# Spreading the zero fill of three pair tables and starting a scatter stream later, in a four-layer graph network

## What is computed

```python
# layer 0, with h = layernorm(x)
msg = relu(h[src] + edge_attr @ We + be)
agg = segment_sum(msg, dst, num_segments=2500)
out = relu(batchnorm((h + agg) @ W + b))
# later layers use the same edges again (list 1), for example
out = segment_sum(h[src] * norm[:, None], dst, num_segments=2500)
# the expert network of layer 2 has attention over the second edge list (list 2)
```

## Time and profile before

| | |
|---|---|
| median of three timed runs | 6236.67 us |
| the profiled execution | 6194.75 us, span 6192.9 us |
| mean granted TensorE clock | 0.877 |
| TensorE busy | 4971.2 us (80%) |
| VectorE busy | 3507.4 us (57%) |
| GpSimd busy | 3159.1 us (51%) |
| ScalarE busy | 1631.4 us (26%) |
| row adds (L776) in the edge stage | 340, the first at 52.5 us, the last at 1465.4 us |

### The profile page before, as it was taken

How to read it: one execution, slowest core, us unless ns; L and a number is a source line. 1 busy time by engine, 2 the same in 40 slices (tenths; PEclk the granted TensorE clock), 3 DMA queues, 4 the chain that set the end, 5 groups by cost and what they waited for, 6 DMA issues and landing times.

```text
span 6192.9 us, 70248 instructions
## 1 busy us (share of the span) xinstructions
PE 4971.2 (80%) x23435; PEld 2959.7 (48%) x23497; DVE 3507.4 (57%) x7225; ACT 1631.4 (26%) x2765; POOL 3159.1 (51%) x2151
## 2 busy tenths in 40 slices
PE   4677767675999888989569796386775998999999
PEld 3444444444555675567566564383222333222266
DVE  5566666654566312120335410399996999777754
ACT  1111111112222102210232211126773001666521
POOL 4578888888888778877778778302220000000000
PEclk8777777776899989999778798698998999999999
DMA  7766666675544785569898776794443110322200
GB/s 203 160 130 117 118 123 113 122 107 65 17 16 13 66 97 16 17 54 110 119 148 100 57 75 39 115 210 111 112 111 79 29 29 21 82 81 81 79 14 27
DMA packets 534579, 523.31 MB, mean 85 GB/s; under 512 B 263641, under 2 KB 489874, under 8 KB 527159
## 3 DMA queue, kind: packets, MB, share of 16 engines
q1 hardware_dynamic: 271560, 427.90, 31.3%
q0 software_dynamic: 261696, 90.13, 23.3%
q10 hardware_dynamic: 1028, 1.52, 0.1%
HBM read 365.58 MB, written 153.75 MB: 84 GB/s over the span
## 4 chain that ended last, share of the span: by engine, by line
POOL 29%; PE 22%; DMA 19%; issue 16%; DVE 10%; SPq 4%; ACT 1%; DVEq 0%; POOLq 0%; ACTq 0%
POOL pairs L724 23%; DMA pairs<-PAIR_CNT,PAIR_IDX 11%; PE PS L2346 6%; PE PS L2183 5%; DMA sums<-WORK,XT 4%; SPq L187 4%; DVE MXS L2224 4%; DVE WORK L1987 4%; POOL sums L776 4%; POOL WORK L763 3%; DMA WORK<-x_table,WORK 3%; PE PS L1011 2%; PE PS L983 2%; PE PS L2204 2%; DVE WORK L1993 1%
## 5 line engine op out<-in xcount | busy, mean ns | idle before, releaser
L724 POOL DMA_INDIRECT pairs<-PAIR_CNT,PAIR_IDX x1364 | 2152.9, 1578 | 563.5 <-issue 421.7
L776 POOL DMA_INDIRECT sums<-WORK,XT x340 | 530.3, 1560 | 213.1 <-issue 113.0
L601 PE MATMUL PS<-WORK,IDENT 125*125 125x256 f32 x680 | 303.0, 538 | 405.9 <-DMA WORK<-x_table,WORK 405.3
L516 DVE SCALAR_TENSOR_TENSOR XT<-PS,ROWS 128x512 f32<-128x512 f32 x704 | 482.6, 746 | 182.7 <-PE PS L502 182.5
L2417 DVE SCALAR_TENSOR_TENSOR WORK<-WORK 125x1000 f32<-125x1000 f32 x400 | 462.3, 1197 | 152.7 <-ACT WORK L2385 151.9
L2183 PE MATMUL PS<-ROWS 32*125 32x500 f32 x3200 | 451.1, 633 | 28.9 <-DVE MXS L2224 19.3
L2224 DVE TENSOR_REDUCE MXS<-PS 125x4 f32<-125x2000 f32 x200 | 438.8, 2235 | 22.4 <-PE PS L2204 18.4
L1627 PE MATMUL PS<-IDENT,WORK 125*125 125x125 f32 x1920 | 259.8, 305 | 238.0 <-DMA WORK<-pairs 159.4
L1661 DVE CUSTOM_DVE_ANT_0 ROWS<-ROWS 125x1250 f32<-125x1250 f32 x200 | 280.8, 1457 | 299.5 <-ACT ROWS L1647 299.5
L644 ACT ACTIVATE WORK<-PS 125x256 f32<-125x256 f32 x340 | 131.0, 385 | 1193.5 <-PE PS L601 1193.5
L2385 ACT ACTIVATE WORK<-PS 125x1000 f32<-125x1000 f32 x400 | 380.0, 1002 | 239.3 <-PE PS L2334 239.3
(11 more groups left out here) (338 smaller groups left out, 8094.6 us busy)
## 6 DMA issues: line engine op xcount, KB each, us to landing
WORK<-pairs SPq DMA_DIRECT2D x400, 218.8 KB
pairs<-ROWS SPq DMA_DIRECT2D x75, 976.6 KB, 7.0
WORK<-pairs SPq DMA_DIRECT2D x48, 1093.8 KB
WORK<-pairs SPq DMA_DIRECT2D x80, 546.9 KB
pairs<-PAIR_CNT,PAIR_IDX POOLq DMA_INDIRECT x1364, 3.6
WORK<-pairs SPq DMA_DIRECT2D x40, 382.8 KB
XT<-pairs SPq DMA_DIRECT2D x12, 1093.8 KB
mask_t<-ROWS SPq DMA_DIRECT2D x40, 273.4 KB
```

The lines of the kernel that those rows point to most:

```text
L516: dve.scalar_tensor_tensor(junk[0:lanes, q, 0:SUPER * lanes], PS[0:lanes, bank, 0:SUPER * lanes], cols[0:lanes, at], weights, ALU.is_equal ...
L601: pe.matmul(PS[0:P, 2 + k % 2, 0:D], IDENT[0:P, 0:P], GATH[0:P, k % 8, :], start=False, stop=True).then_inc(sem("edge_added"), 1)
L724: pool.indirect_dma_start(table, bass.IndirectOffsetOnAxis(idx[:, n:n + 1], 0), cnt[:, n:n + 1], None, compute_op=ALU.add).then_inc(sem(do ...
L776: pool.indirect_dma_start(sums[c], bass.IndirectOffsetOnAxis(SROW[:, k:k + 1], 0), SUMMED[:, k % 8, :], None, compute_op=ALU.add).then_inc ...
```

## The change

Each zero fill still writes the same 1 MB, but its source is now a block of 625 zeros per partition, repeated five times, so that it goes out in 400 packets of 2500 B instead of 80 of 12500 B. The fills are spread evenly over groups 1 to 79, 75/79 per group. The pair adds of the edge stage are still 132, and start from FIRST1 = 112 instead of 68.

```diff
--- before.py
+++ after.py
@@ -473,7 +473,6 @@
         JUNK_LATE = flat(ROWS[:, 3, :], 0, SUPER, SUPER * 128)
 
         ZP, ZL = 25, 80
-        ZERO_FIRST = 13
 
 
         S2, LATE = K2 // SUPER, 80
@@ -530,8 +529,9 @@
                              ).then_inc(sem(f"ea_loaded{g % 2}"), 16)
 
             def zero(table, name, at):
-                sp.dma_start(table[0:PAIRS, :].rearrange("(r p f) o -> r p (f o)", r=ZP, p=ZL)[at],
-                             ZERO[0:ZL, 0:PAIRS // (ZP * ZL)]).then_inc(sem(name), 16)
+                sp.dma_start(table[0:PAIRS, :].rearrange("(r p q f) o -> r p q (f o)", r=ZP, p=ZL, q=5)[at],
+                             ZERO[0:ZL, 0:PAIRS // (ZP * ZL) // 5].unsqueeze(1).to_broadcast([ZL, 5, PAIRS // (ZP * ZL) // 5])
+                             ).then_inc(sem(name), 16)
 
             group(0)
             sp.wait_ge(sem("cleared_zero"), 1)
@@ -547,7 +547,7 @@
             for g in range(1, NG):
                 group(g)
                 done = 3 * ZP - len(zeros)
-                due = min(2 * g, ZP) if g <= ZERO_FIRST else ZP + -(-2 * ZP * (g - ZERO_FIRST) // (NG - 6 - ZERO_FIRST))
+                due = -(-3 * ZP * g // (NG - 6))
                 for _ in range(min(due - done, len(zeros))):
                     zero(*zeros.pop(0))
                 if g == NG - 6:
@@ -718,7 +718,7 @@
             finish(NG - 1, True)
             stage_end(dve)
 
-        FIRST1, EARLY1 = 68, 132
+        FIRST1, EARLY1 = 112, 132
 
         def add_pair(pool, table, done, idx, cnt, n):
             pool.indirect_dma_start(table, bass.IndirectOffsetOnAxis(idx[:, n:n + 1], 0), cnt[:, n:n + 1], None,
```

## The result

The changed kernel takes 6207.84 us (median of six, 6201.53 to 6217.01) against 6235.37 us (six, 6231.49 to 6255.01): 0.9954 of before, interval 0.9938 to 0.9969. Timed once more on another occasion it was 0.9934 (0.9915 to 0.9954), 6203.0 against 6240.3 us. The forecast was 6193 us, between 6155 and 6232: the direction and the range held, the gain was 28 to 37 us where 44 were forecast. Ratios are given with a 95% interval; the quotient of two medians differs from them by up to 0.0015, which is inside every interval.

The account below looks back on a forecast made before the run. GpSimd's queue bounds the edge stage; its waits fall from 85.8 us to 8 + 26 x 1.3 = 41.8, a 44.0 us gain: 6194.75 to 6150.8 us, or 6193 from the timed median; range 6155 to 6232.

Parts of the forecast that it names:

- What bounds the kernel: Edge stage: GpSimd's issue, 3.175 us a tile, plus 85.8 us of waits for landed row adds, sets the pace.
- the signs that the prediction named: Starts: tile 70's row add near 312 us, stage's last row add near 1421, last pair add near 3893.
- The plan: Edge stage: one fill per group, not two in groups 1 to 12; first pair add at tile 113, not 70.
- The backlog at the start: First three groups: three fills at once instead of six, waits 8 us instead of 15.7.
- Behind tile 113: Rest of the edge stage: old waits 7.0 us, no change taken, 0 to -5 us allowed.
- e: Wait that one 1 MB fill costs GpSimd's row adds up to tile 112: taken as 1.3 us, 26 fills.
- The anchor: Whole kernel: gain taken from the profiled 6194.75 us, then 41.9 us added to reach the timed median.
- A: Small packets help little, e from 0.8 to 1.8 us: gain 57 to 31 us, 6180 to 6206 us; chance 0.48.
- B: Small packets help wholly, e near 0 to 0.8 us: gain up to 78 us, 6159 to 6180; chance 0.22.
- C: Edge stage: projection chain takes over at 3.2 us a tile, losing 39 us of gain: 6198 us; chance 0.08.
- D: Later pair-add landings fall worse, or e is 1.8 to 2.9 us: 6206 to 6234 us; chance 0.15.
- E: 2500 B packets hold engines longer, 6.1 us a fill, e = 4.2 us: slower, 6360 us; chance 0.07.

Follow-up runs that it names:

- the second chip: Kernel before and changed kernel, both unedited, traced again on one chip; the kernel before ran in 6239.2 us, waits 78.7 us against 53.0 in the changed one.
- both runs on packets: Changed kernel with 80 packets of 12500 B per fill again: 0.9945 of before; kernel before with 400 packets of 2500 B, old plan: 1.0004.
- the fifths: Changed kernel with each 1 MB fill cut into five DMAs of 200 KB (80 packets of 2500 B), issued tile by tile: 0.9866 of before, 6137.8 us.

## Why the prediction was right, and where it missed

**What bounds the kernel: right.** The edge stage is GpSimd's issue time plus waits for landed row adds, and a microsecond there is handed to the end: 29.2 us at the last row add, 24.5 at the last pair add on one chip, 37 us in its timed medians. Of the signs that the prediction named, tile 70 started at 319.0 us (312 forecast), the last row add at 1432.4 (1421), and the last pair add at 3947.7 (3893): the last miss is 11 us of the stage and 43 us of the scatter behind it.

**The plan: right.** The double groups are gone, the fills' waits are one per group, and tiles 70 to 112 lose their cover, by 17 to 20 us in the run that moves the pair adds alone. The backlog at the start was put at 8 us and is 5.3. SyncE's issue costs 0.6 us a fill as before, so nothing. Behind tile 113 the forecast took no change with 0 to -5 us as its range. Of the 33.0 us at the last row add 28.1 come from the waits; tile 2 is 1.2 us later; so some 6 us come from behind, where the row adds' waits on landings between 500 and 1440 us fell from 8.9 us to 0.6. On the second chip it was 2.4 us.

**e, the cost of one fill, was mis-sized.** The sum put it at 1.3 us between 0 (turns packet by packet) and 1.8 (size doesn't matter), and it is 2.0 and, on the second chip, 1.8 ((53.0 - 5.7) / 26). That term alone is 26 x 0.7 = 18 us, and turns the forecast gain of 44 us into 26 plus the small terms. Those, 2.7 us at the start and 6 behind tile 113, less 1.2 for the later tile 2, gave back 7 to 8 us, which was luck: it is part of why the time stayed within 15 us of the forecast. The row that was set aside as no measurement of e, pair adds landing in 7.7 us among 1 KB packets, pointed the right way, and the end "size doesn't matter" should have been taken as it stood. The experiments put in its place: a row add that meets a 1 MB fill waits for about the fill's whole time on the engines, in 80 packets or in 400.

**The anchor.** The forecast went from the profiled execution to the median by adding 41.9 us. That offset was in the main the scatter of the part from the last row add to the last pair add (2472 us in that trace, 2484 to 2521 in the eleven others), so adding it was right, but a comparison of that trace with the changed kernel's would have shown a loss of 22 us where there is a gain.

**The rivals.** A holds in mechanism, at its far end and just past it (e = 1.8 to 2.0, 6203 and 6208 us; its range ended at 6206). B is refuted by both runs on packets, C by the fifths. D, a fill that costs more than 1.8, holds in its mildest form for the first trace. E is refuted: less 0.4 us for the edge load, a fill held an engine 4.0 us instead of 3.7, and it would have taken 4.9 to make the kernel slower.

The best versions found cut the burst: 0.9861 and 0.9866 of before, at least twice the gain of the change.

## What to carry to other kernels

A bulk transfer that shares the DMA engines with short, latency-bound transfers should be cut until one piece's time on the engines fits into the spare time of the short ones; cutting its packets inside one DMA did nothing that these runs could tell, cutting the DMA and spacing the pieces left 1.3 of the 53 to 58 us of waits. Before spreading work evenly, ask which waits were hidden by work that the same change moves off: here a later start of the pair adds gave back 17 of 40 us. And compare traces of one chip, or more than one trace, before saying where a gain went.

## What was not expected of the hardware

- 16 packets of 12500 B read from 16 neighbouring partitions took 1.38 us each, from every eighth partition 0.69 us, with nothing else changed; in time, 0.9975 against 0.9861 of before.
- Five DMAs of 200 KB in a row took SyncE 3.5 to 4.4 us to issue, one of 1 MB in 400 packets 0.6 us, and one of 200 KB issued tile by tile 0.32 us (the median of 113).
- Two fills of 1 MB queued one behind the other kept GpSimd's queue at 6 packets in 5 us, with no turn for it between them, although a row add had been issued before.
- The part from the last row add to the last pair add, the same instructions in each kernel, took from 2472 to 2521 us in twelve traces. Of the 44 us between the two traces of the kernel before, 28.5 are waits for landings of pair adds.
